# Layer 0 of a two-layer convolution and recurrence kernel: the MLP of a tile moved to other places of the loop, its residual from VectorE to ScalarE and GpSimd

## The chip, the cores and the metric

The kernel runs on one core of a Trainium2 chip. The metric is the device time of one execution in microseconds (us), and lower is better. The engines are PE (TensorE, the matrix engine), DVE (VectorE), ACT (ScalarE), POOL (GpSimd) and SP, which starts the loads and stores. Each has a queue of its own, which it works off in order; engines wait for one another by semaphores.

## What is computed

The input is x with 16 images of 16 x 16 tokens and 96 channels. Two layers follow one another. Layer 0, cut to what matters:

```python
h = layernorm(x, n1_g, n1_b)
p = h @ w_in + b_in                              # 96 -> 192 channels
local = depthwise_conv_3x3(p, k_conv)
lr, rl = ema(local, axis=2), ema(local, axis=2, reverse=True)
tb, bt = ema(local, axis=1), ema(local, axis=1, reverse=True)
mixed = layernorm(0.25 * (lr + rl + tb + bt) + local, on_g, on_b)
x = x + (mixed @ w_out + b_out)                  # 192 -> 96
h2 = layernorm(x, n2_g, n2_b)
x = x + gelu(h2 @ w1 + b1) @ w2 + b2             # 96 -> 384 -> 96
```

Layer 1 is a layer norm, two products (u and a gate g), eight steps of h = g * (h @ A) + (1 - g) * u, a residual, and a second MLP of the same size. The change doesn't touch its code, apart from waits at its start.

## The kernel before

**Tiles.** x is held in SBUF as 8 tiles of two images, 512 tokens each, in four chunks of 128 tokens. Layer 0 is a loop over passes i = -2 to 8 (`body0(i)`, written once for each engine, the first and last passes unrolled). A pass works on several tiles at once, and the names are the same on all engines: n = i + 2 (statistics of the first layer norm, LN1, and its scaling into `xn1`), f = i + 1 (transposes of `xn1` into bank 0, the split of it into a high and a low part `xh1`, `xl1`, and the product with w_in into `pA` or `pM` and bank 1), c = i (the nine taps of the convolution, accumulated in `cA` and `cB`), m = i - 1 (`cA`, `cB` transposed, copied to `local`, the mix of all four scans as a product with the matrix `mix`, its copy `mixed`, six transposes of it, `mcA` and `mcB`, W_out, the residual `x2`, and LN2 into `xn2`), g = i - 2 (transposes of `xn2`, split `xh2`, `xl2`, first MLP product with w1, gelu into `hid`) and e = i - 3 (second MLP product with w2 into bank 7, residual into `x_all`). After pass 8 comes a turn (`turn`), in which the recurrence of tile 0 starts while the last MLPs of layer 0 are finished, and then layer 1's loop.

**PE** (L1310 to L1440 of `body0`) works in each pass through: transposes of `cA`, `cB` (L1333), LN1's transposes (`ln1_transposes`), two thirds of the second MLP product (`mlp2`, L1215), LN2's transposes (`ln2_transposes`), the mix (L1379), the first third of the first MLP product (`mlp1`, L1197 to L1199, three products each: high by high, low by high, high by low), the transposes of `mixed` (L1396, L1398), the second third, W_out (L1414, L1419), the last third, w_in (L1298, L1310), and the first third of `mlp2` of the next tile. In passes 2 and 8 (`mix_first`) LN2's transposes stand behind the mix and the whole of `mlp1` behind W_out.

**ACT** copies from PSUM (`local` L660, `mixed` L698, `mcA` and `mcB` L707 and L708, the splits L536 and L537), scales LN1's output (`normalize1`, L629), applies the first tap (`first_taps`, L650) and the gelus (`gelu0`, L611). One-time work stands between: `setup1` and `setup_m1` in pass 2 (L582 to L595) and `setup2` in pass 3 (L601 to L604).

**DVE** has the statistics (L828, L832, L974, L984), taps 1 to 8 (L933), `x2` (L1002) and the MLP's residual (`residual3`, L874).

**POOL** has the power -0.5 of the variances (`inverse_std`, L367: `rs1`, `rsm`, `rs2`), the low parts of the splits (L364), `xn2` (L374), the additions of a row (`add_row`, L378: `xb` is x plus a bias, used by `x2`; `x_all<-x2,rows` adds the MLP's bias b2), and one-time work (`setup_w1_low` L407, `setup2` L427).

## Time and profile before

| | us |
|---|---|
| Median of 3 runs | 236.05 (235.89 to 236.66) |
| The profiled execution's own time | 236.0 |
| Its span | 234.2 |
| PE busy | 227.3 (97%) |
| DVE busy | 187.3 (80%) |
| ACT busy | 133.5 (57%) |
| POOL busy | 127.7 (55%) |

The profile is of one execution. Its span runs from the first to the last instruction, and 1.8 us of the execution's own time lie around it. Matmuls are pipelined: the profile's duration of one is longer than the distance to the next, so a PE that is busy all the time in the table can still have gaps of some tenths of a us. Where such gaps matter, starts are compared with starts.

The page shows 26% of the chain of work that ended last as "issue", nearly all of it in layer 1, and PE with 43% as the largest engine in it. A line or a time below always belongs to the kernel before, unless it is said otherwise.

### The profile page before, as it was taken

To read this page: it belongs to the slowest core of one execution; us is meant where nothing else is said; L and a number is where in the kernel's file an instruction comes from. 1 tells how busy PE (TensorE), PEld (TensorE's weight loads), DVE (VectorE), ACT (ScalarE), POOL (GpSimd) and SP (SyncE) were. 2 spreads that over 40 slices of the span, in tenths; PEclk is the share of its full clock that TensorE was granted. 3 is DMA by queue.
4 is the path that set the end of the run, shared out by engine and by line. 5 is a ranking of instruction groups with operands and counts; after the bars stand their busy time and mean duration, and the time that the engine had idled before them with its cause. 6 is when DMAs were issued, how large, how long until landed. Compare 5 with 4: busy or idle time off the path is not lost.

```text
span 234.2 us, 4144 instructions
## 1 busy us (share of the span) xinstructions
PE 227.3 (97%) x1376; PEld 184.9 (79%) x1376; DVE 187.3 (80%) x470; ACT 133.5 (57%) x301; POOL 127.7 (55%) x161
## 2 busy tenths in 40 slices
PE   8999899999999999999999999999999999999995
PEld 5796867969697978887787887878788887978685
DVE  7799998999999999995458688696968778686741
ACT  5667886767675866455923937264372727353252
POOL 6564777887859392938677351526335351516130
PEclk9999999999999999999999999999999999999999
DMA  3951000000000000000000000010101001010102
GB/s 107 231 168 36 1 0 0 4 0 0 3 1 0 3 1 0 3 0 0 0 3 1 0 3 0 0 35 4 34 1 34 3 0 34 3 34 0 35 3 67
DMA packets 5637, 4.99 MB, mean 21 GB/s; under 512 B 528, under 2 KB 5360, under 8 KB 5616
## 3 DMA queue, kind: packets, MB, share of 16 engines
q1 hardware_dynamic: 5328, 4.64, 6.9%
q8 instruction: 11, 0.18, 0.3%
q10 hardware_dynamic: 288, 0.09, 0.2%
q14 instruction: 10, 0.08, 0.1%
HBM read 3.15 MB, written 1.57 MB: 20 GB/s over the span
## 4 chain that ended last, share of the span: by engine, by line
PE 43%; issue 26%; POOL 17%; DMA 5%; DVE 5%; ACT 2%; SPq 1%; POOLq 0%; DVEq 0%; ACTq 0%
PE pM L1215 8%; PE bank L1379 8%; POOL hs L493 8%; POOL rs L367 6%; DMA x_all<-in_x 5%; PE bank L1414 3%; POOL x4b L378 3%; PE pM L1197 3%; PE bank L1184 3%; PE bank L1419 2%; PE bank L1333 2%; PE bank L1310 2%; PE pM L1199 2%; PE pM L1198 2%; DVE cA L933 2%
## 5 line engine op out<-in xcount | busy, mean ns | idle before, releaser
L367 POOL TENSOR_TENSOR rs<-var,power 128x4 f32<-128x4 f32 x32 | 32.5, 1016 | 47.4 <-DVE var L832 43.9
L933 DVE SCALAR_TENSOR_TENSOR cA<-pA,cols,cA 128x528 f32<-128x528 f32 x54 | 40.8, 756 | 0.4
L1514 PEld LDWEIGHTS pM<-w,hid 128*128 128x128 f32 x168 | 27.3, 191 | 3.5
L1260 PE MATMUL pA<-q,a_half 96*96 96x256 f32 x96 | 27.1, 381 | 0.3 <-DVE q L1015 0.3
L1514 PE MATMUL pM<-w,hid 128*128 128x96 f32 x168 | 26.9, 263 | 0.0
L933 DVE SCALAR_TENSOR_TENSOR cB<-bank,cols,cB 128x256 f32<-128x256 f32 x56 | 26.5, 473 | 0.0
L1015 DVE SCALAR_TENSOR_TENSOR q<-th,bank 96x256 f32<-96x256 f32 x48 | 19.8, 416 | 7.6 <-PE bank L1260 7.3
L1215 PEld LDWEIGHTS pM<-w,hid 128*128 128x128 f32 x192 | 24.4, 192 | 0.9
L1215 PE MATMUL pM<-w,hid 128*128 128x96 f32 x192 | 24.8, 271 | 0.0
L1184 PE MATMUL bank<-ident,xn 128*96 128x128 f32 x120 | 23.3, 273 | 0.0
L364 POOL TENSOR_TENSOR xl<-xc,xh 96x512 fp32r<-96x512 f32 x15 | 19.1, 1275 | 5.7 <-ACT xh L537 4.8
L1379 PE MATMUL bank<-local,mix 128*128 128x384 f32 x64 | 22.1, 488 | 0.0
L809 ACT ACTIVATE xh<-bank 96x512 fp32r<-96x512 f32 x7 | 4.2, 593 | 26.6 <-PE bank L1184 26.6
L611 ACT ACTIVATE hid<-pM,bias 128x512 f32<-128x512 f32 x23 | 15.2, 688 | 5.9 <-PE pM L1199 5.6
L1379 PEld LDWEIGHTS bank<-local,mix 128*128 128x128 f32 x64 | 11.6, 190 | 6.7 <-issue 0.2
L1184 PEld LDWEIGHTS bank<-ident,xn 128*96 128x96 f32 x120 | 14.9, 136 | 1.9 <-issue 0.6
L1260 PEld LDWEIGHTS pA<-q,a_half 96*96 96x96 f32 x96 | 13.2, 163 | 3.1 <-DVE q L1015 1.1
L1015 DVE SCALAR_TENSOR_TENSOR q_three<-th,pA 96x256 f32<-96x256 f32 x16 | 6.7, 417 | 10.7 <-PE pA L1260 9.7
L493 POOL TENSOR_TENSOR hs<-hs,q_three 96x512 f32<-96x512 f32 x8 | 10.2, 1270 | 9.0 <-DVE q_three L1015 9.0
L374 POOL TENSOR_SCALAR xn<-x,ng,rs 128x96 f32<-128x96 f32 x32 | 13.1, 424 | 1.7 <-POOL rs L367 1.6
L1015 DVE SCALAR_TENSOR_TENSOR q<-th,pA 96x256 f32<-96x256 f32 x32 | 12.6, 413 | 1.5 <-PE pA L1260 0.8
L698 ACT ACTIVATE mixed<-bank 128x384 f32<-128x384 f32 x16 | 7.9, 491 | 9.1 <-PE bank L1379 9.1
(245 smaller groups left out, 579.7 us busy)
## 6 DMA issues: line engine op xcount, KB each, us to landing
x_all<-in_x SPq DMA_DIRECT2D x8, 192.0 KB, 2.9
out<-y SPq DMA_DIRECT2D x7, 192.0 KB, 2.0
w<-in_w SPq DMA_DIRECT2D x1, 480.0 KB, 6.0
w<-in_w SPq DMA_DIRECT2D x1, 336.0 KB, 3.3
mix<-in_mix SPq DMA_DIRECT2D x1, 256.0 KB, 3.5
out<-y SPq DMA_DIRECT2D x2, 96.0 KB, 1.7
...
```

Source lines behind the costliest of these rows:

```text
L364: return pool.tensor_tensor(lo[0:D, :], v[0:D, :], hi[0:D, :].bitcast(F32), ALU.subtract)
L367: pool.tensor_tensor(rs[:, :], var[:, :], power[:, :], ALU.pow).then_inc(step, 1)
L374: pool.tensor_scalar(xn[:, k * D:(k + 1) * D], v[:, k * D:(k + 1) * D], ng[:, k:k + 1], rs[:, k:k + 1], ALU.add, ALU.mult).then_inc(ready, 1)
L493: pool.tensor_tensor(hs[c % 2][0:D, :], hs[c % 2][0:D, :], moved(c, k)[0:D, :], ALU.add)\
L611: act.activation(hid[:, j * TILE:(j + 1) * TILE], bank[banks[j]][:, :], ACT.Gelu, bias=B[f"b1_{j}"]).then_inc(s["gelu_done"], 1)
L933: dve.scalar_tensor_tensor(out=acc, in0=src, scalar=col(f"k{'AB'[grp]}{k}"), in1=acc, op0=ALU.mult, op1=ALU.add).then_inc(s["conv_step"], 1)
L1015: dve.scalar_tensor_tensor(out=moved(c, k + 1)[0:D, half(h)], in0=th[c % 2][0:D, half(h)], scalar=1.0, in1=step_bank(k, h), op0=ALU.add, o ...
L1184: last = pe.transpose(dst[0:D, k * P:(k + 1) * P], src[:, k * D:(k + 1) * D], ident[:, :])
L1215: last = pe.matmul(psum[:, k * D:(k + 1) * D], hid[:, j * TILE + k * P:j * TILE + (k + 1) * P], wc0("w2", j * D, (j + 1) * D), start=(j == ...
L1260: pe.matmul(step_bank(k, h), a_half[0:D, :], moved(c, k)[0:D, half(h)], start=k not in (1, 3), stop=True, skip_group_check=True)\
L1379: last = pe.matmul(bank[4 + a][:, 0:384], mix[:, k * TOKENS + a * P:k * TOKENS + (a + 1) * P], local[:, k * 384:(k + 1) * 384], start=(k = ...
L1514: last = pe.matmul(bank[V_BANK][:, k * D:(k + 1) * D], hid1[:, j * TILE + k * P:j * TILE + (k + 1) * P], wc1("m2", j * D, (j + 1) * D), st ...
```

## The change

**What it does.** In layer 0's loop:

- PE: LN2's transposes move behind the mix in all passes. `mlp1` moves to the end of the pass, behind W_out and w_in, and its third part goes to bank 0 instead of bank 6. Inside `mlp1` the product with `xl2` comes third instead of second, with the wait for `xl2` in front of it. `mlp2` is no longer begun in the pass before: its 12 chunk products (24 matmul instructions in the trace) are put between the LN1 transposes, the halves of the mix, the LN2 transposes, and four of them behind the transposes of `mixed`. `ln2_bank` is bank 6 instead of bank 0.
- Since the third part of `mlp1` is in bank 0, LN1's transposes (bank 0 too) wait for the third gelu of the tile (`gelu_done`), and so do layer 1's first transposes in pass 8 (`ln3_transposes(0)`).
- ACT: `normalize1` moves forward, behind the split of the tile f and, in pass 2, ahead of `setup1`. The split of `xn2` moves behind `mcB`, and the three gelus to the end of the pass, behind `first_taps`. `mcA` waits for the first four transposes of `mixed` only. A new copy of bank 7 to `xr` follows `mcB`.
- POOL: `rs1` moves to the start of the pass, `xb` is made in the pass that uses it, `xl2` moves behind `rsm` (and, in pass 3, behind `setup2`), and a new addition `x_all<-xr,x_all` follows.
- DVE: the residual L874 leaves layer 0's loop (it stays for the last two tiles, which are finished in the turn and behind it).

The core of the diff:

```diff
         def ln2_bank(t):
-            return bank[1 if t >= TILES - 2 else 0]
+            return bank[1 if is_last(t) else 6]
...
@@ POOL, body0 @@
-                if peeled(i, 1):
+                if tile_known(n) and not peeled(i, 0):
                     ln1_std()
...
-                if tile_known(g):
-                    pool.wait_ge(s["x2_split"], 2 * g + 2)
-                    wait(pool, s["hid_psum"], 3 * g)
-                    split_low(xl2, xc2, xh2).then_inc(s["x2_lo"], 1)
+                if tile_known(m):
+
+                    pool.wait_ge(*x_landed(m))
...
+                    wait(pool, s["x2_ready"], 4 * m)
+                    add_row(xb[:, :], x_tile(m), brow[:, :], s["xb_ready"])
...
                     if peeled(i, 3):
                         setup2()
+                    if tile_known(g):
+                        ln2_low()
+                    if tile_known(e):
+                        pool.wait_ge(s["xr_ready"], e + 1)
+                        pool.wait_ge(s["x2b_ready"], e + 1)
+                        pool.tensor_tensor(x_tile(e), xr[:, :], x_tile(e), ALU.add).then_inc(s["x3_ready"], 1)
...
@@ ACT, body0 @@
+                if i >= 2:
+                    normalize1(n)
                 if peeled(i, 2):
                     setup1()
                     setup_m1()
...
+                if tile_known(e) and i <= TILES:
+                    act.wait_ge(s["w2_done"], e + 1)
+                    wait(act, s["x3_ready"], e)
+                    act.activation(xr[:, :], bank[7][:, 0:384], ACT.Copy).then_inc(s["xr_ready"], 1)
+                if tile_known(g) and not is_last(g):
+                    split2()
...
@@ DVE, body0 @@
-                if tile_known(e):
-                    residual3(e, bank[7])
...
@@ PE, body0 @@
+                    if f >= 4:
+                        pe.wait_ge(s["gelu_done"], 3 * (f - 3))
...
+                if tile_known(g) and not is_last(g):
+                    if peeled(g, 0):
+                        pe.wait_ge(s["w1_high"], 2)
+                        pe.wait_ge(s["w1_low"], 1)
+                    mlp1(g, 0, bank[6])
+                    wait(pe, s["xr_ready"], g)
+                    mlp1(g, 1, bank[7])
+                    if peeled(i, TILES):
+                        pe.wait_ge(s["x3_lo"], 1)
+                    else:
+                        pe.wait_ge(s["x2_ready"], 4 * m + 4)
+                    mlp1(g, 2, bank[0])
```

**Where the order moves.** On POOL, from the end of pass 1 to the middle of pass 2, this stands before (`xn2` here is tile 0's, the last `rs1` tile 4's):

```order
L378 TENSOR_TENSOR xb<-x_all,brow 128x384 [waits brow_ready,wo_ready]
L367 TENSOR_TENSOR rs1<-var1,power 128x4 [waits xn1_ready,var1_ready]
L364 TENSOR_TENSOR xl1<-xc1,xh1 96x512 [waits p_psum,x1_split]
L367 TENSOR_TENSOR rsm<-varm,power 128x4 [waits varm_ready]
L407 TENSOR_TENSOR w1_l<-w1_f,w1_h 96x384 [waits w1_high]
L370 TENSOR_TENSOR ng2<-st2,minus 128x4 [waits var2_ready]
L367 TENSOR_TENSOR rs2<-var2,power 128x4
L374 TENSOR_SCALAR xn2<-x2,ng2,rs2 128x96 [waits ln2_step]
L374 TENSOR_SCALAR xn2<-x2,ng2,rs2 128x96 x3
L378 TENSOR_TENSOR xb<-x_all,brow 128x384 [waits x2_ready,x_odd_loaded]
L364 TENSOR_TENSOR xl1<-xc1,xh1 96x512 [waits p_psum,x1_split]
```

And in the changed kernel:

```order
L364 TENSOR_TENSOR rs1<-var1,power 128x4 [waits xn1_ready,var1_ready,wo_ready]
L361 TENSOR_TENSOR xl1<-xc1,xh1 96x512 [waits p_psum,x1_split]
L375 TENSOR_TENSOR xb<-x_all,brow 128x384 [waits brow_ready,x_even_loaded]
L364 TENSOR_TENSOR rsm<-varm,power 128x4 [waits varm_ready]
L404 TENSOR_TENSOR w1_l<-w1_f,w1_h 96x384 [waits w1_high]
L367 TENSOR_TENSOR ng2<-st2,minus 128x4 [waits var2_ready]
L364 TENSOR_TENSOR rs2<-var2,power 128x4
L371 TENSOR_SCALAR xn2<-x2,ng2,rs2 128x96 [waits ln2_step]
L371 TENSOR_SCALAR xn2<-x2,ng2,rs2 128x96 x3
L364 TENSOR_TENSOR rs1<-var1,power 128x4 [waits xn1_ready,var1_ready]
L361 TENSOR_TENSOR xl1<-xc1,xh1 96x512 [waits p_psum,x1_split]
```

`xb` of tile 0 now stands between `xl1` and `rsm`, and tile 4's `rs1` right behind tile 0's `xn2`.

On ACT, pass 2, from the split of tile 3 to the copy of the mix, the changed kernel has this. Before, the two rows of `xn1` stood behind the first two gelus, and the others were in this order:

```order
L544 ACTIVATE xh1<-bank0 96x2x2x128
L636 ACTIVATE xn1<-x_all,rs1 128x96 [waits trx_done,x_even_loaded,ln1_step]
L636 ACTIVATE xn1<-x_all,rs1 128x96 x3
L589 ACTIVATE a_half<-w1 96x96 [waits w1_loaded]
L593 ACTIVATE bias<-pM,cols 96x1 [waits l1_psum]
L593 ACTIVATE bias<-pM,cols 96x1
L596 ACTIVATE bias<-pM,cols 128x1 x3
L598 ACTIVATE ug_f<-pM 96x192
L602 ACTIVATE m1_f<-pM 96x384 [waits l1_psum]
L707 ACTIVATE mixed<-bank4 128x384 [waits mix_done,varm_ready,mtr_done]
L707 ACTIVATE mixed<-bank5 128x384 [waits mix_done]
```

`ln1_step` is what `rs1` on POOL signals, so the six one-time copies and both `mixed` now stand behind a wait for POOL.

On PE, pass 7, the changed kernel has this at the end, from the last W_out product to the transposes of pass 8; before, two of the three MLP parts stood ahead of W_out and the third right behind it:

```order
L1442 MATMUL bank0<-woBB,mcB 128x2x96
L1217 MATMUL pM<-xh2,w1_h 128x512 [waits gelu_done,x2_split]
L1218 MATMUL pM<-xh2,w1_l 128x512
L1221 MATMUL pM<-xl2,w1_h 128x512 [waits x2_lo]
L1217 MATMUL pM<-xh2,w1_h 128x512 [waits xr_ready]
L1218 MATMUL pM<-xh2,w1_l 128x512
L1221 MATMUL pM<-xl2,w1_h 128x512
L1217 MATMUL bank0<-xh2,w1_h 128x512 [waits x2_ready]
L1218 MATMUL bank0<-xh2,w1_l 128x512
L1221 MATMUL bank0<-xl2,w1_h 128x512
```

In passes 2 to 6 the twelve products of w_in (L1315, L1327 there) stand between W_out and these rows; in pass 7 there are none, since no tile is left for w_in.

## Rows read from the trace of the kernel before

**Rows 1.** Busy time by window, one a pass: length, then each engine's, then granted clock.

```profile
27.63:41.99 14.36, 13.45 (x86) 10.79 (x84) 13.59 (x36) 10.52 (x28) 9.82 (x14) 1.00 0.00 1
41.99:55.22 13.23, 13.21 (x88) 10.81 (x86) 12.66 (x31) 9.53 (x24) 10.88 (x15) 1.00 0.00 1
...
68.21:81.23 13.02, 13.02 (x87) 10.84 (x86) 12.38 (x29) 8.94 (x19) 9.21 (x13) 1.00 0.01 2
...
94.23:105.30 11.07, 11.07 (x72) 8.93 (x70) 10.97 (x25) 5.63 (x12) 7.29 (x10) 1.00 0.01 1
105.30:117.64 12.34, 12.06 (x74) 9.50 (x73) 6.03 (x17) 8.86 (x22) 8.40 (x11) 1.00 0.00 0
```

**Rows 2.** PE's timeline in pass 5: start us, us, operation.

```profile
68.21 0.60 PE L1333 MATMUL bank<-ident,cA 128*128 128x128 f32 x4
...
68.86 0.60 PE L1184 MATMUL bank<-ident,xn 128*96 128x128 f32 x4
...
74.27 0.51 PE L1197 MATMUL pM<-xh,w_h 96*128 96x512 f32 x1
...
76.59 1.13 PE L1414 MATMUL bank<-woA,mcA 128*128 128x96 f32 x8
...
78.93 0.41 PE L1298 MATMUL pA<-xh,wi_h 97*128 97x256 f32 x2
...
80.37 1.03 PE L1215 MATMUL pM<-w,hid 128*128 128x96 f32 x8
81.23 0.49 PE L1333 MATMUL bank<-ident,cA 128*128 128x128 f32 x3
```

**Rows 3.** ACT's timeline in pass 5.

```profile
79.13 0.69 ACT L611 ACTIVATE hid<-pM,bias 128x512 f32<-128x512 f32 x1
```

**Rows 4.** DVE's timeline in pass 5.

```profile
71.33 0.56 DVE L874 TENSOR_TENSOR x_all<-pM,x_all 128x384 f32<-128x384 f32 x1
...
78.53 0.99 DVE L1002 SCALAR_TENSOR_TENSOR x<-bank,rsm,xb 128x96 f32<-128x96 f32 x4 [0.31 <-PE bank L1419]
```

**Rows 5.** POOL's timeline in passes 1 and 2.

```profile
25.38 1.01 POOL L367 TENSOR_TENSOR rsm<-varm,power 128x4 f32<-128x4 f32 x1
...
29.88 1.66 POOL L374 TENSOR_SCALAR xn<-x,ng,rs 128x96 f32<-128x96 f32 x4
31.51 1.00 POOL L378 TENSOR_TENSOR xb<-x_all,brow 128x384 f32<-128x384 f32 x1
```

**Rows 6.** ACT's timeline in pass 2.

```profile
30.25 0.29 ACT L582 ACTIVATE a_half<-w 96x96 f32<-96x96 f32 x1
...
31.34 0.53 ACT L595 ACTIVATE m_f<-pM 96x384 f32<-96x384 f32 x1
...
33.49 0.49 ACT L698 ACTIVATE mixed<-bank 128x384 f32<-128x384 f32 x1 [0.72 <-PE bank L1379]
```

**Rows 7.** DVE's timeline in pass 2.

```profile
34.38 0.55 DVE L974 BATCH_NORM_STATS2 stm<-mixed 128x6 f32<-128x384 f32 x1
...
37.64 0.75 DVE L933 SCALAR_TENSOR_TENSOR cA<-pA,cols,cA 128x528 f32<-128x528 f32 x1
```

**Rows 8.** The one-time work of pass 3 on ACT.

```profile
50.55 0.29 ACT L601 ACTIVATE bias<-bias 96x1 f32<-96x1 f32 x2
...
50.99 0.51 ACT L604 ACTIVATE m_h<-m_f 96x384 fp32r<-96x384 f32 x1
```

**Rows 9.** The same on POOL, and a low part of the split.

```profile
52.16 1.01 POOL L427 TENSOR_TENSOR m_l<-m_f,m_h 96x384 fp32r<-96x384 f32 x1
...
72.94 1.27 POOL L364 TENSOR_TENSOR xl<-xc,xh 96x512 fp32r<-96x512 f32 x1 [0.24 <-ACT xh L537]
```

**Rows 10.** ACT's timeline at the change from pass 7 to pass 8.

```profile
105.22 1.16 ACT L753 ACTIVATE xn<-x_all,rs 128x96 f32<-128x96 f32 x4
```

**Rows 11.** PE's timeline in layer 1, where transposes and pairs of products alternate.

```profile
133.00 0.27 PE L1184 MATMUL bank<-ident,xn 128*96 128x128 f32 x1
...
133.31 0.27 PE L1184 MATMUL bank<-ident,xn 128*96 128x128 f32 x1
```

More of the change, by code:

```diff
@@ L177, in build @@
         xb, x2 = sb("xb", CHUNKS * D), sb("x2", CHUNKS * D)
+        xr = sb("xr", CHUNKS * D)
         hid = sb("hid", HJ * TILE)
@@ L436, in ln1_std, with ln2_low @@
                     inverse_std(rs1, var1, s["ln1_step"])
-                if peeled(i, 1):
+                def ln2_low():
+                    pool.wait_ge(s["x2_split"], 2 * g + 2)
+                    wait(pool, s["hid_psum"], 3 * g)
+                    split_low(xl2, xc2, xh2).then_inc(s["x2_lo"], 1)
+                if tile_known(n) and not peeled(i, 0):
                     ln1_std()
@@ L1206, in mlp1 @@
                 w = slice(P * j, P * (j + 1))
-                three_passes(psum[:, :], w1_h[0:D, w], w1_l[0:D, w], xh2[0:D, :], xl2[0:D, :])\
-                    .then_inc(s["hid_psum"], 1)
+                pe.matmul(psum[:, :], w1_h[0:D, w], xh2[0:D, :], start=True, stop=False)
+                pe.matmul(psum[:, :], w1_l[0:D, w], xh2[0:D, :], start=False, stop=False)
+                if j == 0:
+                    pe.wait_ge(s["x2_lo"], g + 1)
+                pe.matmul(psum[:, :], w1_h[0:D, w], xl2[0:D, :], start=False, stop=True)\
+                  .then_inc(s["hid_psum"], 1)
             def mlp2(e, j, psum, parts=range(CHUNKS)):
@@ L1316, in body0, with last_mlp @@
                 f, m, g, e = i + 1, i - 1, i - 2, i - 3
+                def last_mlp(*places):
+                    for at in places:
+                        if tile_known(e):
+                            mlp2(e, at // CHUNKS, bank[7], [at % CHUNKS])
                 if peeled(i, -2):
                     keep_warm(WARM_UP)
-                if tile_known(e):
-                    mlp2(e, 0, bank[7])
                 if tile_known(m):
@@ L1352, in ln1_transposes @@
                     else:
-                        transposes(bank[0], xn1, s["trx_done"])
+                        for k in range(CHUNKS):
+                            transposes(bank[0], xn1, s["trx_done"], [k])
+                            between(k)
                 if peeled(i, 0):
@@ L1361, in body0 @@
                 elif tile_known(f):
-                    ln1_transposes()
+                    ln1_transposes(last_mlp)
+                else:
+                    for k in range(CHUNKS):
+                        if peeled(i, TILES):
+                            ln3_transposes(0, [k])
+                        last_mlp(k)
                 if peeled(i, 2):
@@ L1365, in body0 @@
                     setup2()
-                if tile_known(e):
-                    mlp2(e, 1, bank[7])
-                    mlp2(e, 2, bank[7])
-                if peeled(i, TILES):
-                    ln3_transposes(0)
-                if tile_known(g) and not mix_first(g):
-                    ln2_transposes(g)
                 if tile_known(m):
@@ L1384, in body0 @@
                     ln1_transposes()
-                if mix_first(g):
-                    ln2_transposes(g)
-                mlp1_now = tile_known(g) and not is_last(g)
-                if mlp1_now and not mix_first(g):
-                    mlp1(g, 0, bank[6])
+                for k in range(CHUNKS):
+                    if tile_known(g):
+                        ln2_transposes(g, [k])
+                    if k < 2:
+                        last_mlp(6 + k)
                 if tile_known(m):
@@ L1395, in body0 @@
                             k = 2 * im + a
-                            pe.transpose(bank[4][:, k * P:(k + 1) * P], src, ident[:, :])
+                            last = pe.transpose(bank[4][:, k * P:(k + 1) * P], src, ident[:, :])
+                    last.then_inc(s["mtr_done"], 1)
                     for a in range(2):
@@ L1403, in body0 @@
                     gu(0, 1)
-                if mlp1_now and not mix_first(g):
-                    wait(pe, s["x3_ready"], g)
-                    mlp1(g, 1, bank[7])
                 if tile_known(m):
```

82 lines of the change are left out of this document (36 added, 46 removed).

## The prediction, made before the changed kernel was run

> **What bounds the kernel now.** I read the windows first, pass by pass, then PE's timeline inside one pass, then the rows of the other engines at the places where PE waits. A full pass of layer 0 takes 13.02 us and PE is busy in all of it, the clock granted in full; DVE has 12.38 us of it [rows 1]. So layer 0 is PE's. Comparing starts shows what little is left: in pass 5 PE waits about 0.08 us for LN2's transposes, 0.21 us before the first MLP part at 74.27 and 0.25 us before W_out at 76.59 [rows 2]. That is 0.54 us, so PE's own work in a full pass is 12.48 us. DVE is close behind but does wait for PE: 0.31 us before `x2` [rows 4]. By the same comparison of starts PE's gaps in passes 2 to 8 are 1.65, 0.75, 0.51, 0.54, 0.52, 0.47 and 0.75 us, together 5.2 of the 90.0 us from the first to the last of these windows. Layer 1 follows at its own pace, and its recurrence starts as soon as PE has worked off pass 8. What passes 2 to 8 gain or lose is therefore gained or lost in the end.
>
> **The removed and added work.** No matmul is added or taken away. DVE loses one residual a tile for six tiles, 0.56 us each [rows 4], which counts nothing while DVE waits for PE. ACT gets a copy of 128x384 from PSUM, 0.49 us like that of the mix [rows 6], and POOL an addition of 128x384, between 1.00 (one operand a repeated row, [rows 5]) and 1.27 us (two full operands of 96x512, [rows 9]); I take 1.0. In a middle pass both have room for it. Twelve chunk products now alternate with transposes and mix halves. The nearest rows are layer 1's, a transpose and two trace instructions of a product in 133.31 - 133.00 = 0.31 us [rows 11], against 0.11 + 2 x 0.11 = 0.33 from groups of one kind (0.60 us of transposes take 0.44 by starts; eight instructions 81.23 - 80.37 = 0.86 [rows 2]). So alternating costs nothing; between -0.02 and +0.02 us each it is 0.2 us a pass at most either way.
>
> The Trainium skill (SBUF — State Buffer, on the two separate sides) says that a GpSimd instruction and a VectorE instruction with two SBUF inputs hold one port pair in turn and block each other. By that rule an addition of two SBUF tiles on POOL might hold DVE up by up to its 1.0 us. In layer 0 DVE's taps and `x2` read one operand from PSUM, so the rule asks nothing here, and by it the sum is the same.
>
> **Where the waits go, pass by pass.** I use four latencies, as starts show them: PE's end to ACT's start 0.20 us (the MLP part ends where the next product starts, 78.93, and the gelu starts at 79.13 [rows 2, 3]), ACT's end to PE about 0.1, POOL to ACT or PE 0.05 to 0.1, PE to DVE 0.3.
>
> *Middle passes (4, 5, 6; the same wait also in 3 and 8).* `mlp1` is now last in the pass, and its third part is in bank 0, which LN1's transposes of the next pass need. Between them PE has only the transposes of `cA` and `cB`, 68.86 - 68.21 = 0.65 us. The third gelu starts 0.20 us after the third part, lasts 0.69 [rows 3], and PE goes on about 0.09 later: 0.98 us after the end of `mlp1`, a wait of 0.33. ACT is free for the gelus, since the taps' copies end 0.2 us earlier. The other waits are covered. The low part of the split is asked for 3.4 us after `mlp2`'s end, and xr 0.2 + 0.49, split 1.1, `xl2` 1.27 make 3.1; the copy `mixed` (0.2 + 0.49 after the mix) is under 0.88 us of LN2 transposes and products; `mcA` is under the last four products. DVE's tap 8 ends about 0.9 us before w_in asks. So 12.48 + 0.33 = 12.81 us a pass, and three passes gain 0.2 each: **-0.6**.
>
> *Pass 2.* This is the largest term. `xn1` of tile 4 now stands on ACT ahead of `setup1` and of `mixed`, and waits for `rs1`, which stands on POOL behind tile 0's `xn2`. `xn2` needs `x2`, `x2` needs `rsm`, and `xb` (1.0 us, about 0.6 of it new delay) is put ahead of `rsm`: it started at 25.38 [rows 5] and now at 26.0, so `x2` and all after it come 0.4 later. `xn2` ended at 31.5 and now at 32.0; `rs1` takes 1.0: 33.0. Then ACT: `xn1` 1.1 (34.1), the six one-time copies from 30.25 to 31.34 + 0.53, so 1.6 (35.7), two `mixed` 0.9 (36.6). The second `mixed` ended at 33.98 [rows 6]: 2.6 later. PE, done with the mix at 33.3, stands until 35.8 for LN2's transposes (bank 6 must have been read by `setup1`), then takes the transposes of `mixed` at 36.65 and W_out at 38.0, done at 39.6. DVE waits for `mixed` too: its statistics start at 36.2, and tap 8 on `cA` ends 37.64 + 0.75 - 34.38 = 4.0 later [rows 7], at 40.2. w_in starts at 40.3 instead of right behind W_out. With 1.42 of w_in and 2.1 of `mlp1` the pass ends at 43.84. Before, it ended at 41.99 with 0.87 of `mlp2` in it that is now in pass 3; that compares 43.84 with 41.12: **+2.7**.
>
> *Pass 3.* `setup2` stands on ACT behind the copy to `xr` and the split, and on POOL ahead of `xl2`. From 43.84 on: `mlp2` ends at 51.56 (with the gelu's wait of 0.33), `xr` 51.76 to 52.25, the split to 53.2, on ACT `setup2` (50.99 + 0.51 - 50.55 = 0.95 [rows 8]) to 54.1, on POOL `ug_l` and `m1_l` (1.0 [rows 9], from 54.3) to 55.3 and `xl2` to 56.6. PE comes to the first product with `xl2` at 55.0 and gets it at 56.7: 1.7 of wait. With 0.33 that is 2.05 against 0.75 before: **+1.3**.
>
> *Pass 7.* There is no w_in any more, so `mlp1` comes right behind W_out while its split has only just begun: `mlp2` ends at 7.3 us of the pass, W_out at 8.85, the split at 9.05 (`xr` is ahead of it), `xl2` at 10.4. PE waits 0.35 for the split and 0.9 for the low part. The late gelu also delays `local` and with it the mix by 0.35. Together 1.6 against 0.47: **+1.1**.
>
> *Pass 8.* Layer 1's first transposes wait for their `xn3`, which ACT makes behind the three gelus. The gelus are now last in pass 7: 0.20 + 0.69 after the pass ends, then 1.16 for the four scalings [rows 10] less the 0.1 by which neighbours overlap, so PE goes on 2.04 us into the pass, where it would have been there at 0.65. All of `mlp2` stands behind these transposes. 1.4 against 0.75 before, since the old gap at the MLP goes: **+0.6**.
>
> **The sum** is -0.6 + 2.7 + 1.3 + 1.1 + 0.6 = +5.1, unrounded +5.2. The recurrence starts at about 122.8 instead of 117.64 [rows 1]. Against the profiled execution's own 236.0 us that is 241.2; the median 236.05 is the same within its spread.
>
> **Rivals.** (1) *DVE was the real pace.* If the 0.56 us residual counts in full, passes 3 to 6 fall by 0.54 each (PE's own work is the floor) and the added waits are passed under other work: 236.0 - 2.2 = 233.8, faster. For it speaks that DVE has 12.38 of 13.02 us; against it the 0.31 us that DVE waits for PE, and that the waits in passes 2, 3, 7 and 8 follow from the queues' order. It decides if `rs1` of tile 4 is there when ACT has done the split in pass 2 (30.4); my chain has it at 33.0, so 2.6 us would have to be wrong. (2) *The waits at the end don't bind:* the copy to `xr`, split and low part in pass 7 are ready sooner, or what pass 8 loses is given back in the turn, where PE, DVE and POOL alternate: without the 1.7 us of passes 7 and 8, and with a middle pass of 12.6, 239.0. (3) *The clock falls.* PE stands 2.5 us in pass 2, where before no gap in a pass was above 0.7, and the granted clock was 1.00 in every window [rows 1]. At half the clock the 7 us of PE work that follow cost up to 3.5 more: 244; a middle value is 243.5. The Trainium skill (TensorE: Matmul & The Clock Gate, part 1) has it that the throttled rate is the default and that activity releases it; no run here shows it yet, and by that page a long enough stand in pass 2 would give just this. (4) *Nothing measurable:* pass 2's and 3's waits are half hidden and the middle passes gain more: about 236, which has no mechanism of its own in the rows.
>
> **Chances.** The forecast (239.8 to 242.8) 0.74, rival 2 (238 to 239.8) 0.10, the clock 0.08, rival 1 0.05, rival 4 0.03. The range reaches from 239.2 to 243.0: at its low end most of the waits of pass 7 or 8 are gone, at the high end alternating costs 0.2 a pass and the addition on POOL 1.27. A measurement of this kernel can tell 0.3% (0.7 us) from no change. Faster by more 0.05, within it 0.03, slower 0.92.
>
> **What the changed profile would show.** Passes 4 to 6 at 12.8 us each, with PE's wait for the gelu in front of LN1's transposes; 12.5 would say that the bank's wait is covered, 13.0 that something else came. In pass 2 `rs1` at about 32 on POOL, ACT idle from 30.4 to 33, `mixed` at 35.7 and PE idle from 33.3 to 35.8. In pass 3 a wait of PE for POOL's `xl2` of 1.7 us, in pass 7 one of 0.9, in pass 8 one of 1.4 for ACT's `xn3`. Layer 1's tiles keep their distance. The prediction is wrong if the start of the recurrence moves by less than 3 us, or if layer 1 gets shorter.

## The result, and the profile after

Before: 236.73 us, median of 6 executions (235.89 to 237.09). After: 242.95 us, median of 6 (241.07 to 243.6). The changed kernel takes 1.025 times as long, 95% interval 1.021 to 1.029. The profiled execution of after took 241.07 us, 5.1 more than the one of before; its span is 239.3 us and its granted clock 1.00. In the other executions the clock is lower in most, which is a cost of its own (below).

The windows, one a pass, as in [rows 1] (length, then busy time of PE, its weight loads, DVE, ACT and POOL, then the granted clock). The rows are passes 2, 3, 4, 7 and 8 (5 and 6 are as long as 4):

```profile
28.41:44.02 15.61, 12.77 (x78) 9.85 (x77) 14.23 (x37) 10.00 (x27) 10.39 (x14) 1.00 0.00 0
44.02:58.46 14.44, 12.82 (x87) 10.69 (x86) 13.53 (x33) 10.26 (x25) 11.41 (x15) 1.00 0.01 2
58.46:71.22 12.76, 12.55 (x86) 10.77 (x85) 10.83 (x26) 9.40 (x21) 10.35 (x14) 1.00 0.00 1
...
96.74:108.81 12.07, 11.36 (x71) 8.99 (x69) 11.83 (x29) 6.17 (x13) 8.72 (x13) 1.00 0.01 1
108.81:122.53 13.72, 12.54 (x81) 10.35 (x79) 4.11 (x11) 9.94 (x24) 8.68 (x11) 1.00 0.01 1
```

In a middle pass PE is busy for 12.55 us where it was 13.02, and the pass is 0.26 shorter: the change does there what it is made for. Passes 2, 3, 7 and 8 lose more than that. Where, the list of PE's waits from pass 1 to the end of pass 8 shows (us in total, times, longest):

```profile
PE pM L1221 <- POOL xl L361: 2.0, 2, 1.4
PE pM L1195 <- ACT m_f L602: 1.9, 1, 1.9
PE bank L1195 <- ACT xn L765: 1.2, 1, 1.2
...
PE bank L1195 <- ACT hid L618: 0.9, 4, 0.2
PE bank L1327 <- DVE cB L946: 0.8, 1, 0.8
PE pA L1315 <- DVE cA L946: 0.4, 1, 0.4
```

None of these is in before, but for the waits for `mcA` that are left out here. L1221 is the product with `xl2` in passes 3 and 7, L1195 the transposes: of LN2 in pass 2, of layer 1 in pass 8, of LN1 in passes 3 to 6 (0.2 us by the list, 0.37 by starts).

Pass 2, the largest. POOL's and ACT's timelines in after, then PE's:

```profile
25.06 1.01 POOL L375 TENSOR_TENSOR xb<-x_all,brow 128x384 f32<-128x384 f32 x1
26.17 1.02 POOL L364 TENSOR_TENSOR rsm<-varm,power 128x4 f32<-128x4 f32 x1
...
30.67 1.67 POOL L371 TENSOR_SCALAR xn<-x,ng,rs 128x96 f32<-128x96 f32 x4
32.31 1.00 POOL L364 TENSOR_TENSOR rs<-var,power 128x4 f32<-128x4 f32 x1
```

```profile
33.35 1.17 ACT L636 ACTIVATE xn<-x_all,rs 128x96 f32<-128x96 f32 x4 [2.18 <-POOL rs L364]
...
35.52 0.49 ACT L602 ACTIVATE m_f<-pM 96x384 f32<-96x384 f32 x1
35.90 0.87 ACT L707 ACTIVATE mixed<-bank 128x384 f32<-128x384 f32 x2
```

```profile
36.16 0.62 PE L1195 MATMUL pM<-ident,xn 128*96 128x128 f32 x4 [1.93 <-ACT m_f L602]
...
38.16 1.13 PE L1437 MATMUL bank<-woA,mcA 128*128 128x96 f32 x8 [0.47 <-ACT mcA L714]
...
40.38 0.51 PE L1315 MATMUL pA<-xh,wi_h 97*128 97x256 f32 x2 [0.41 <-DVE cA L946]
```

`xb` now starts where `rsm` started [rows 5], and everything down the chain is later: ACT stands 2.18 us for `rs1` of tile 4, the second `mixed` ends at 36.77 instead of 33.98 [rows 6], and PE, which could go on at 34.2, goes on at 36.16.

Pass 3. `setup2` on POOL (L424) stands ahead of the low part, and PE waits:

```profile
53.86 0.60 POOL L424 TENSOR_TENSOR ug_l<-ug_f,ug_h 96x192 fp32r<-96x192 f32 x1 [1.03 <-ACT ug_h L610]
54.42 1.01 POOL L424 TENSOR_TENSOR m_l<-m_f,m_h 96x384 fp32r<-96x384 f32 x1
55.40 1.26 POOL L361 TENSOR_TENSOR xl<-xc,xh 96x512 fp32r<-96x512 f32 x1
```

```profile
56.71 0.50 PE L1221 MATMUL pM<-xl,w_h 96*128 96x512 f32 x1 [1.40 <-POOL xl L361]
```

And PE in passes 7 and 8:

```profile
107.06 0.51 PE L1221 MATMUL pM<-xl,w_h 96*128 96x512 f32 x1 [0.62 <-POOL xl L361]
...
110.81 0.32 PE L1195 MATMUL bank<-ident,xn 128*96 128x128 f32 x1 [1.18 <-ACT xn L765]
```

The recurrence starts at 122.53 instead of 117.64, +4.89. From there to the end of the span it was 116.56 us and is 116.77, so layer 1 is as it was.

### The profile page after: what moved, and what is told of

Read it like the earlier page. It is cut to its first block, busy times and chain, and to the rows that moved or that the text cites. A ratio compares the mean times of both kernels' runs of the same rounds, so it can differ in the third digit from the quotient of the medians.

```text
span 239.3 us, 4158 instructions
## 1 busy us (share of the span) xinstructions
PE 225.9 (94%) x1376; PEld 184.7 (77%) x1376; DVE 186.1 (78%) x464; ACT 137.0 (57%) x307; POOL 134.0 (56%) x167
## 4 chain that ended last, share of the span: by engine, by line
PE 32%; issue 29%; POOL 23%; DVE 8%; ACT 7%; POOLq 0%; DVEq 0%; ACTq 0%
POOL rs L364 8%; POOL hs L500 7%; PE pM L1229 6%; PE bank L1402 6%; ACT hid L618 4%; POOL x4b L375 3%; DVE cA L946 3%; PE bank L1143 2%; PE bank L1195 2%; PE bank L1437 1%; DVE cB L946 1%; PE bank L1442 1%; POOL xn L371 1%; POOL xl L361 1%; PE bank L1277 1%
## 5 line engine op out<-in xcount | busy, mean ns | idle before, releaser
L1229 PEld LDWEIGHTS pM<-w,hid 128*128 128x128 f32 x192 | 28.4, 192 | 5.2 <-issue 1.2
L1538 PEld LDWEIGHTS pM<-w,hid 128*128 128x128 f32 x168 | 27.3, 191 | 3.5
L1229 PE MATMUL pM<-w,hid 128*128 128x96 f32 x192 | 29.0, 265 | 0.0
L1538 PE MATMUL pM<-w,hid 128*128 128x96 f32 x168 | 26.9, 263 | 0.0
L1402 PE MATMUL bank<-local,mix 128*128 128x384 f32 x64 | 24.6, 497 | 0.1
L1195 PE MATMUL bank<-ident,xn 128*96 128x128 f32 x92 | 21.6, 274 | 2.0 <-ACT xn L765 1.2
L1195 PEld LDWEIGHTS bank<-ident,xn 128*96 128x96 f32 x92 | 12.7, 143 | 4.2 <-issue 1.9
L364 POOL TENSOR_TENSOR rsm<-varm,power 128x4 f32<-128x4 f32 x8 | 8.2, 1019 | 12.8 <-DVE varm L995 12.7
L618 ACT ACTIVATE hid<-pM,bias 128x512 f32<-128x512 f32 x16 | 10.7, 687 | 5.2 <-PE pM L1221 5.0
L1402 PEld LDWEIGHTS bank<-local,mix 128*128 128x128 f32 x64 | 10.7, 191 | 3.8 <-ACT local L667 0.3
```

Source lines behind the costliest of these rows:

```text
L364: pool.tensor_tensor(rs[:, :], var[:, :], power[:, :], ALU.pow).then_inc(step, 1)
L618: act.activation(hid[:, j * TILE:(j + 1) * TILE], bank[banks[j]][:, :], ACT.Gelu, bias=B[f"b1_{j}"]).then_inc(s["gelu_done"], 1)
L1195: last = pe.transpose(dst[0:D, k * P:(k + 1) * P], src[:, k * D:(k + 1) * D], ident[:, :])
L1229: last = pe.matmul(psum[:, k * D:(k + 1) * D], hid[:, j * TILE + k * P:j * TILE + (k + 1) * P], wc0("w2", j * D, (j + 1) * D), start=(j == ...
L1402: last = pe.matmul(bank[4 + a][:, 0:384], mix[:, k * TOKENS + a * P:k * TOKENS + (a + 1) * P], local[:, k * 384:(k + 1) * 384], start=(k = ...
L1538: last = pe.matmul(bank[V_BANK][:, k * D:(k + 1) * D], hid1[:, j * TILE + k * P:j * TILE + (k + 1) * P], wc1("m2", j * D, (j + 1) * D), st ...
```

## The experiments

All runs of a group share their runs of before. Its medians were 236.39 (first group, with `again`, `warm`, `ln1_late`, `xb_back`), 236.15 (second, with `setup2_p4`, `two_ahead`, `tail8`, `tail7`) and 236.66 us (third). Since the granted clock differs from one execution to the next, I give the time at each clock.

**The changed kernel again.**

> The changed kernel itself, to see its spread. Its runs so far fall into two groups, 241.1 to 241.4 us with a mean granted clock of 1.00 and 243.0 to 243.6 us with 0.986 to 0.993. Theory (clock): PE stands about 2.1 us in pass 2, and in some executions the clock then falls for some us; so again two groups, 241.2 and 243.1, and the kernel before shows 1.00 in all its runs. If a profile shows the lower clock, PEclk drops in a stretch that begins near pass 2 (34 to 36 us). Rival (place by chance): the lower clock shows in runs of the kernel before as well, and its place has nothing to do with the stand in pass 2.

Measured: 242.92 us, ratio 1.027 (1.022 to 1.031). One by one: 240.82 at clock 1.00; 242.83, 242.92 and 242.93 at 0.993; 244.24 at 0.984; 245.4 at 0.977. With the first six there are three executions at 1.00 (240.82 to 241.35), four at 0.993 (242.83 to 242.95), four at 0.984 to 0.986 (242.96 to 244.24) and one at 0.977. The profiled one here was at 0.993. In its windows of 1 us (columns as above) the clock is at half, 1.2 GHz, from about 57.4 to 60.8:

```profile
56.00:57.00 1.00, 0.00 (x0) 0.00 (x0) 1.00 (x3) 0.00 (x0) 1.00 (x1) 1.00 0.00 0
57.00:58.00 1.00, 0.82 (x2) 0.70 (x3) 1.00 (x3) 0.06 (x1) 1.00 (x2) 0.68 0.00 0
58.00:59.00 1.00, 1.00 (x4) 0.73 (x3) 1.00 (x3) 0.63 (x1) 1.00 (x3) 0.50 0.00 0
...
60.00:61.00 1.00, 1.00 (x6) 0.80 (x6) 1.00 (x3) 0.56 (x1) 1.00 (x4) 0.62 0.00 0
61.00:62.00 1.00, 1.00 (x10) 0.81 (x9) 1.00 (x3) 0.80 (x3) 0.97 (x2) 1.00 0.00 0
```

Ahead of it stands PE's wait for `xl2` in pass 3, 1.42 us in this trace (56 to 57 holds no matmul at all). So the fall has a place, and I had not named it: my clock rival spoke of pass 2 alone. By the Trainium skill (TensorE: Matmul & The Clock Gate, part 1) the throttled rate is the default and activity releases it. These rows agree: half the clock behind a stand, the full one again with PE busy.

**Pass 2's stand filled with matmuls of no use.**

```
+if peeled(i, 2):
+    pe.wait_ge(s["x1_split"], 8)
+    keep_warm(4, bank[0])
 for k in range(CHUNKS):
     if tile_known(g):
         ln2_transposes(g, [k])
```

> The changed kernel with four matmuls of ones into bank 0 put into PE's stand in pass 2, ahead of LN2's transposes; 4 x 0.43 = 1.7 us of work into 2.1 us of idle time, nothing waits for them. Theory (clock): the granted clock is 1.00 in all runs and the median is that of the fast group, 241.1 us (LN2's transposes start at 36.16 as they do now). Rival: the two groups stay, since the fall comes from something else, and the median stays near 243.

Measured: 241.18 us, ratio 1.022 (1.019 to 1.026). Four executions at 1.00 (240.85 to 241.23) and two at 0.993 (242.85, 242.95); none at 0.986 or below. The stand in front of LN2's transposes is 0.64 us instead of 1.93, PE's times are otherwise the same. The time is the expected one, the full clock in all executions is not there. Six executions alone don't settle which fall belongs to which stand; the profiles of the runs below do: those at 0.993 have one fall behind pass 3's stand, the one at 0.986 one behind pass 2's, those at 0.978 and 0.979 both.

**LN1 of tile 4 in its old place, behind `mixed`.**

```
 act, ahead of the setup:             act, at the end of the pass:
-if i >= 2: normalize1(n)            -if i < 2 and ...: normalize1(n)
+if i >= 3: normalize1(n)            +if i < 3 and ...: normalize1(n)
```

> The changed kernel with one move undone: in pass 2 ACT scales tile 4's LN1 behind the gelu inputs again (ahead of the first taps), not ahead of the one-time copies. My account of pass 2: ACT no longer waits for POOL's rs1 at 30.5 to 33.3, LN2's transposes start at 34.1 instead of 36.2, and then DVE sets the pace: its statistics of the mix start at 35.2 instead of 36.4, w_in at 39.2 instead of 40.4. So 1.2 us less, not 2.1: 239.9 at full clock. PE's longest stand in pass 2 is then below 1 us, so by the clock theory all runs have a clock of 1.00. Rival (the wait doesn't matter, PE's other waits take its place): 241.1.

Measured: 241.11 us, ratio 1.020 (1.018 to 1.022); all four executions at 0.993, with the low clock behind pass 3's stand again (0.74 in 57 to 58, 0.50 in 58 to 59). LN2's transposes start at 34.63 with no wait, and W_out at 36.72. Then one wait has become another:

```profile
36.72 1.13 PE L1437 MATMUL bank<-woA,mcA 128*128 128x96 f32 x8 [0.47 <-ACT mcA L714]
...
39.69 0.50 PE L1315 MATMUL pA<-xh,wi_h 97*128 97x256 f32 x2 [1.16 <-DVE cA L946]
```

Pass 2 takes 43.29 - 28.98 = 14.31 us instead of 15.61, 1.3 less where 1.2 was expected. The median is 1.8 us below `again`'s executions at the same clock; no row here places the 0.5 between the two. The expected gain is there, the expected full clock is not, and DVE's tap leaves a stand of 1.16 us where none above 1 was expected.

**`xb` of tile 0 in its old place, at the end of POOL's pass 0 and ahead of `rsm`.**

```
 pool, ahead of rsm:                  pool, behind setup_w_out() of pass 0:
-if tile_known(m):                        +pool.wait_ge(s["brow_ready"], 1)
+if tile_known(m) and not peeled(m, 0):   +add_row(xb, x_tile(0), brow, s["xb_ready"])
     add_row(xb, x_tile(m), brow, s["xb_ready"])
```

> The changed kernel with tile 0's row addition xb where it was, ahead of rs1 of tile 3 at the end of POOL's pass 0. Theory (port): in the changed kernel DVE's varm of pass 1 lasts 0.90 instead of 0.26 us and ends 0.02 us after POOL's xb (25.06 to 26.07); it is held until that ends. With xb gone from there varm lasts about 0.3 and ends with xl1 on POOL, w_in's second half starts 0.8 us earlier (26.8), x2 of tile 0 starts at 26.7 instead of 27.5, and the whole chain of pass 2 (rs1, LN1's scaling, the mix) comes 0.8 earlier: 240.3 at full clock. Rival (queue only, what I had predicted): rsm alone was late, x2 comes 0.4 earlier, 240.7, and varm keeps its 0.9.

Measured: 240.17, 240.24 and 240.32 us at 1.00, 243.37 and 243.47 at 0.986, 243.82 at 0.977; median 241.85, ratio 1.022 (1.017 to 1.027). At the full clock this is 0.6 to 0.8 us below the changed kernel, and nearer to the 240.3 of the port theory than to its rival's 240.7. `varm` took 0.15 us, which decides between them. `xb` starts at 22.11 (22.05 in the kernel before), `x2` at 26.80 instead of 27.47, and pass 3 at 43.30 instead of 44.02. Three executions of six still fall, as both stands are still there (1.89 and 1.40 us).

**`setup2` on POOL one pass later.**

```
 pool:
+if peeled(i, 4):
+    setup2()
 pool.wait_ge(s["varm_ready"], m + 1)
...
-if peeled(i, 3):
-    setup2()
 ln2_low()
```

> The changed kernel with one thing moved: POOL's setup2 (ug_l and m_l of layer 1) goes from pass 3, ahead of the low part of LN2, to the start of pass 4, ahead of rsm. Theory: in pass 3 the first MLP products wait 1.4 us for POOL's low part, because setup2's two operations stand ahead of it (0.60 and 1.01 us long). Without them that wait is gone, the pass is about 12.9 instead of 14.4 us, and the whole is 1.6 us shorter: 239.4 us at the clock of 1.00 (the changed kernel at that clock: 240.8 to 241.4). Pass 4 gets nothing, because POOL waits for varm there. The same stand of PE in pass 3 is what the clock falls behind in the executions at 0.993, so fewer of them should fall than of the changed kernel: most at 1.00, the rest with one fall and 241.3. Rival: POOL is then late for rsm of pass 4 by 1.6 us, x2 and with it the product W_out come later, and the time only moves from pass 3 to pass 4: 241.0 us.

Measured: 239.58 us, ratio 1.017 (1.012 to 1.021); five executions at 0.998 to 1.00 (239.23 to 240.26) and one of 242.78 at 0.986. PE goes through the products with `xl2` of pass 3 without a wait, the pass takes 57.44 - 44.69 = 12.75 us instead of 14.44, and pass 4 12.98, 0.2 longer: 1.5 us less in the trace. Against their own runs of before the executions at the full clock are 3.3 us above (239.42 - 236.15), `again`'s was 4.4: 1.2 less. Of the rival's return in pass 4 only 0.2 us came. No execution shows 0.993 any more. My price for the one that fell, 241.3, was too low: at 0.986, the mark of a fall behind pass 2's stand, it costs 3.3.

**Two products of the second MLP ahead of LN1's transposes.**

```
-ln1_transposes(last_mlp)
+last_mlp(0, 1)
+ln1_transposes(lambda k: last_mlp(k) if k > 1 else None)
```

> The changed kernel with PE's order of the second MLP product changed: in passes 2 to 7 two of its products stand ahead of LN1's transposes and the rest among them, where all stood among the transposes. Theory: in each middle pass PE waits 0.33 us for the third gelu or for the bank it frees, and two products more ahead of that point hide it: 0.3 us in each of four passes, 1.3 us in all, 239.8 us at a clock of 1.00. Rival: the wait isn't at that place or LN1's transposes now come too late for DVE's copy cA and for the projection behind it: a wait of 0.2 to 0.5 us moves there, 241.0 to 242 us.

Measured: 239.46 us at 0.998; 241.84 at 0.993, 242.89 at 0.986, 243.08 at 0.978; median 242.36, ratio 1.022 (1.016 to 1.027). At the full clock this is 3.3 us above its runs of before, 1.1 less than `again`'s 4.4, where 1.3 was expected. Passes 5 and 6 of its trace:

```profile
73.95:86.35 12.40, 12.40 (x87) 10.81 (x86) 12.15 (x30) 9.54 (x21) 10.30 (x14) 1.00 0.01 3
86.35:98.74 12.39, 12.39 (x87) 10.81 (x85) 11.59 (x29) 8.49 (x17) 9.28 (x13) 1.00 0.00 0
```

A middle pass is 0.37 shorter than after's 12.76, and PE is busy in all of it: the wait for the gelu in bank 0 was real, 0.37 us a pass, and could be covered. In this profile, at 0.978, the clock was at half from 36.0 to 42.9 and again from 59.9 to 63.3, behind both stands. And pass 2's stand is longer than in `after`:

```profile
36.10 1.06 PE L1195 MATMUL pM<-ident,xn 128*96 128x128 f32 x4 [2.38 <-ACT m_f L602]
```

**Six products ahead of layer 1's first transposes in pass 8.**

```
+elif peeled(i, TILES):
+    last_mlp(0, 1, 2, 3, 4, 5)
+    ln3_transposes(0)
```

> The changed kernel with PE's order in pass 8 changed: six of the second MLP products stand ahead of layer 1's first transposes. Theory: PE waits there 1.18 us for ACT's xn of layer 1, and products that don't need it can fill that time: the recurrence starts 1.2 us earlier, 239.8 us at a clock of 1.00. Rival: the products wait for gelu themselves (0.69 us each on ACT, which is behind xn), so that what is gained at the transposes is lost at the products: 241 us.

Measured: 240.2 us at 1.00, 242.0 and 242.07 at 0.993, 244.07 at 0.986; median 242.04, ratio 1.022 (1.018 to 1.026). PE has no wait at these transposes any more, and pass 8 takes 125.51 - 112.69 = 12.82 us instead of 13.72. That is 0.9 of the 1.2 expected. The rest has become the next wait: by starts, PE now stands 0.27 us before the mix, which starts at 115.44, for ACT's `local`, which ends at 115.39. Its profile shows the clock at 0.50 from 39.5 to 46.3, 1.8 us behind pass 2's stand (2.38 us here too), and 1.00 behind pass 3's, which is there too (1.40 us).

**Split and low part first in pass 7.**

```
 act:  +if peeled(i, TILES - 1): split2()     # ahead of the copy to xr
 pool: +if peeled(i, TILES - 1): ln2_low()    # ahead of rsm
```

> The changed kernel with two operations moved in pass 7: on ACT LN2's split stands ahead of the residual's copy, on POOL LN2's low part ahead of rsm. Theory: PE waits 0.62 us for POOL's low part, and more for the split behind the mix, since both stand behind other work; with both moved up these waits go, 0.6 to 1.1 us, 240.0 us at a clock of 1.00. Rival: rsm, now later by 1.27 us, holds the values of tile 7's x2, and with them its mix and layer 1's beginning: 241 to 242 us.

Measured: 241.41 us at 1.00, three of 243.19 to 243.31 at 0.992 to 0.993; median 243.24, ratio 1.027 (1.023 to 1.031). No gain, and pass 7 takes 111.05 - 98.57 = 12.48 us instead of 12.07. The rival held:

```profile
106.86 1.28 POOL L361 TENSOR_TENSOR xl<-xc,xh 96x512 fp32r<-96x512 f32 x1 [3.40 <-ACT xh L546]
108.10 1.01 POOL L364 TENSOR_TENSOR rsm<-varm,power 128x4 f32<-128x4 f32 x1
109.20 0.99 DVE L1017 SCALAR_TENSOR_TENSOR x<-bank,rsm,xb 128x96 f32<-128x96 f32 x4 [1.42 <-POOL rsm L364]
110.25 0.50 PE L1221 MATMUL bank<-xh,w_h 96*128 96x512 f32 x1 [0.86 <-DVE x L1017]
```

`rsm` comes later, `x2` with it, and the third part of `mlp1` waits for `x2`. Whichever of the two POOL does first, PE waits for the other.

**The residual alone, in the kernel before.**

```
 dve:  -residual3(e, bank[7])
 act:  +act.activation(xr, bank[7][:, 0:384], ACT.Copy)
 pool: +pool.tensor_tensor(x_tile(e), xr, x_tile(e), ALU.add)
 pe:   wait(pe, s["x3_ready"], g)  ->  wait(pe, s["xr_ready"], g)
```

> The kernel before with the third part of the change alone: the residual's sum leaves DVE, ACT copies bank 7 to SBUF and POOL adds x. PE's order and everything else as before. Theory: in a middle pass DVE waits for PE (0.31 us ahead of x2) and PE never waits for DVE, so 0.56 us less on DVE brings nothing, and the two operations put on ACT and POOL cost nothing either, as both have idle time: 236.2 us, within 0.5. Rival: DVE is what a pass waits for, 0.56 us in each of four passes: 234.0 us. Second rival: POOL's 1.0 us in front of LN2's step makes PE wait for xn, a few tenths a pass: 237 to 238 us.

Measured: 236.87 us, ratio 1.0024 (0.9998 to 1.0050). A middle pass is as it was in [rows 1], with DVE 0.43 us less busy:

```profile
69.11:82.10 12.99, 12.99 (x87) 10.84 (x87) 11.95 (x28) 9.41 (x20) 10.21 (x14) 1.00 0.01 3
```

DVE is not what layer 0 waits for, and this third of the change gains nothing.

**Pass 2's stand filled and `setup2` moved.**

> The changed kernel with setup2 in pass 4 and the four matmuls without use in pass 2's stand. Theory: the clock falls behind the stands of PE in pass 2 and pass 3 and nowhere else; with both filled or gone all six executions show 1.00, and the time is that of setup2_p4 at that clock, 239.3 to 239.7 us. Rival: falls have another cause (the chip, the moment), then one or two of the six show 0.993 or 0.986 here too, at 1.9 us each.

The edits are those of `warm` and of `setup2_p4`. Measured: 240.11 us, ratio 1.015 (1.012 to 1.018), all five executions at 1.00 (239.27 to 240.24). With the 0.5 us by which before was slower here than beside `setup2_p4` taken off this is 239.6, within the expected 239.3 to 239.7. With the stands filled or gone, no execution of this kernel falls, nor one of `five_moves` below. They are not the only cause there is: before itself showed 0.979 and 0.978 in two of its 45 executions of the three groups (241.96 and 242.09 us), and the residual alone 0.993 in one of twelve.

**POOL's addition with one SBUF input.**

```
-pool.tensor_tensor(x_tile(e), xr, x_tile(e), ALU.add)
+pool.tensor_scalar(x_tile(e), xr, 1.0, None, ALU.mult)
```

> The changed kernel with POOL's sum of the residual turned into an operation with one SBUF input (xr times 1, so the sum with x is left out) in the same place. DVE's var2 runs beside it in passes 3 to 7, and took 0.64, 0.39 and 0.38 us where it takes 0.15 to 0.17 alone, with its end at the end of POOL's operation. Theory: a DVE operation from SBUF to SBUF is held until POOL's running operation ends because that one reads two SBUF inputs; with one input it isn't held, and var2 takes 0.15 to 0.17 us in every pass. Rival: any POOL operation holds it, or it waits for something else: 0.4 to 0.6 us stays. The whole time tells nothing here.

The kernel leaves out x in the sum, so its result is wrong and its time tells nothing (one execution, 244.1 us at 0.979). What it is about: DVE's `varm` and `var`, a tensor_scalar of 128x4 from SBUF to SBUF, take 0.15 to 0.17 us. In after, the one at the end of pass 1 took 0.90, and one in each of passes 3 to 7 took 0.38 to 0.64. DVE's rows of after:

```profile
25.19 0.90 DVE L995 TENSOR_SCALAR varm<-stm 128x4 f32<-128x4 f32 x1
...
95.31 0.39 DVE L844 TENSOR_SCALAR var<-st 128x4 f32<-128x4 f32 x1
```

The first ends at 26.09, POOL's `xb` (in the rows of pass 2 above) at 26.07. The last ends at 95.70, and POOL's addition, in its timeline, at 95.67:

```profile
94.65 1.02 POOL L477 TENSOR_TENSOR x_all<-xr,x_all 128x384 f32<-128x384 f32 x1
```

The kernel before had the hold already, 0.1 us of it, at the end of pass 1, DVE's operation ending 0.04 behind POOL's:

```profile
25.05 0.26 DVE L984 TENSOR_SCALAR varm<-stm 128x4 f32<-128x4 f32 x1
```

```profile
24.00 1.27 POOL L364 TENSOR_TENSOR xl<-xc,xh 96x512 fp32r<-96x512 f32 x1
```

Measured with one input: `var` takes 0.17 us in the middle of POOL's operation in passes 4 to 7. Pass 5, DVE and POOL:

```profile
85.54 0.17 DVE L844 TENSOR_SCALAR var<-st 128x4 f32<-128x4 f32 x1
```

```profile
84.92 1.18 POOL L477 TENSOR_SCALAR x_all<-xr 128x384 f32<-128x384 f32 x1
```

One `var` in the same trace fell beside POOL's `m_l` (56.22 to 57.22) and `xl2`, both with two SBUF inputs:

```profile
57.12 1.35 DVE L844 TENSOR_SCALAR var<-st 128x4 f32<-128x4 f32 x1
```

```profile
57.19 1.26 POOL L361 TENSOR_TENSOR xl<-xc,xh 96x512 fp32r<-96x512 f32 x1
```

It ends at 58.47, POOL's at 58.45. So it is held until a POOL addition or subtraction of two full tiles from SBUF ends, and not by one with a single input. The number of inputs alone doesn't decide, though. After has a `var` inside POOL's power of 128x4, which has two SBUF inputs and lasts 1.02 us, and it isn't held:

```profile
96.26 0.17 DVE L844 TENSOR_SCALAR var<-st 128x4 f32<-128x4 f32 x1
```

```profile
95.92 1.02 POOL L364 TENSOR_TENSOR rs<-var,power 128x4 f32<-128x4 f32 x1
```

Whether the small size or the operation makes that difference, no run separates.

Nor is `varm` held in each execution: it depends on which of the two starts first. In the profiles of `after`, `again`, `ln1_late`, `setup2_p4`, `tail7` and `warm_p4` it starts 0.13 to 0.16 us behind `xb` and takes 0.87 to 0.90 us; in those of `warm`, `tail8` and `one_input` it starts 0.14 to 0.21 ahead of it, in `two_ahead` at the same time within 0.01, and takes 0.15 to 0.29. What the hold costs at the end of pass 1 is little: in `warm` POOL's `xb` started later (25.45), `varm` took 0.28, and from the start of pass 1 to that of pass 3 it is 44.07 - 16.87 = 27.20 us against 44.02 - 16.50 = 27.52 in after. 0.3 us, of the 0.8 by which pass 2 starts late.

**Five moves together.**

> The changed kernel with five moves together, each of them tried alone before: LN1 of pass 2 kept in the old place (ln1_late), the first tile's xb behind rsm (xb_back), setup2 in pass 4 (setup2_p4), two products of the second MLP ahead of LN1's transposes (two_ahead), six ahead of layer 1's first transposes in pass 8 (tail8). Theory: the costs lie in different places and add up. From 241.0 us of the changed kernel at a clock of 1.00: 1.7 less in pass 2, perhaps 0.4 more of xb, 1.5 for setup2, 1.5 for the products, 0.85 in pass 8: 235.1 us, and with no long stand of PE left the clock stays at 1.00 in nearly all executions. Rival: the moves overlap, since a wait that is taken away shows the next one behind it, and half is kept: 238 us.

The edits are those of `ln1_late`, `xb_back` (`xb` at the end of pass 0, so ahead of `rsm` and not behind it), `setup2_p4`, `two_ahead` and `tail8`. Measured: 235.65 us, median of 12 executions (235.13 to 236.33), ratio to before 0.9959 (0.9939 to 0.9978), the clock at 0.998 to 1.00 in all twelve. Passes 2 to 4, 7 and 8:

```profile
28.62:43.04 14.42, 12.54 (x77) 9.89 (x76) 14.21 (x37) 10.08 (x27) 10.36 (x14) 1.00 0.00 0
43.04:55.45 12.41, 12.41 (x87) 10.82 (x85) 11.89 (x29) 10.29 (x25) 10.06 (x13) 1.00 0.01 2
55.45:68.04 12.59, 12.59 (x86) 10.79 (x85) 12.45 (x31) 9.53 (x21) 12.00 (x16) 1.00 0.00 1
...
92.86:104.94 12.08, 11.37 (x71) 8.99 (x70) 11.84 (x29) 6.18 (x13) 8.73 (x13) 1.00 0.01 1
104.94:117.76 12.82, 12.71 (x80) 10.48 (x79) 4.09 (x11) 9.90 (x24) 8.69 (x11) 1.00 0.00 1
```

This is the only kernel here that beats before, by 0.4%, which is little but clear of its interval, and it is some 7 us below the median of the changed one. The costs lay in different places and nearly add up (5.4 us below the changed kernel at the full clock, both against their own runs of before, where 5.95 was expected). Passes 3 to 6 are now 0.4 to 0.8 us shorter than before's, together 2.4. Passes 2 and 8 can't be compared by their windows: before began each tile's second MLP product in the pass ahead (0.87 us), so its pass 2 had that part more than this one's and its pass 8 that part less. With it moved, pass 8 is 12.82 us against 13.21, 0.4 shorter, and pass 2 14.42 against 13.49, 0.9 longer. Pass 7 is 1.0 longer, and so the three give 1.5 of the 2.4 back. Pass 2 is DVE's: it is busy for 14.21 of 14.42 us, and PE waits 1.26 for its tap.

## Why the prediction was right, and where it wasn't

The forecast was 241.2 us in 239.2 to 243.0; the median is 242.95. It is inside by 0.05 us, and that is luck: the high end was explained by 0.2 us a pass for alternating and by an addition of 1.27 us on POOL, and neither came (the middle pass is 12.76, the addition 1.02). The 0.74 was given to 239.8 to 242.8, and the median lies above that, on the way to the clock rival's 243.5. An execution at the full clock takes what was forecast (240.82, 241.07 and 241.35). The rest is the clock, which the forecast itself did not contain. Step by step, at the full clock, with the predicted lengths of passes 3, 7 and 8 worked out from the lengths before and the forecast's terms (pass 8's with the 0.87 us of `mlp2` that is now in it):

| | predicted, us | measured, us |
|---|---|---|
| Start of pass 2 | 27.63 | 28.41 |
| Start of pass 3 (term +2.7) | 43.84 | 44.02 (+2.9) |
| Length of pass 3 (+1.3) | 14.5 | 14.44 (+1.2) |
| Middle pass (-0.6 for three) | 12.81 | 12.76 (-0.7) |
| Length of pass 7 (+1.1) | 12.2 | 12.07 (+1.0) |
| Length of pass 8 (+0.6) | 13.8 | 13.72 (+0.5) |
| Start of the recurrence | 122.8 | 122.53 |
| Layer 1 | as before | +0.2 |

- **Middle passes: right.** PE's own work was taken as 12.48 and the wait for the third gelu as 0.33. `two_ahead` has passes of 12.40 and 12.39 without the wait, and the wait is 0.37.
- **Pass 2: right in mechanism and within 0.2 us, with one thing missed.** The chain was forecast link by link: `rs1` done 33.0 (33.31), `mixed` 35.7 (35.90), PE back at 35.8 (36.16), W_out 38.0 (38.16), w_in 40.3 (40.38). Undoing either link gave its part: `ln1_late` and `xb_back`. One statement in it was wrong: that nothing of the shared port is asked for in layer 0, since taps and `x2` read PSUM. DVE's `varm` and `var` go from SBUF to SBUF, and `xb`, moved beside `varm`, holds it for 0.75 us. I had looked at DVE's long operations and not at its short ones, though before's row of `varm` showed 0.26 us where 0.15 is usual. Where `varm` is held it delays the start of pass 2 by 0.8 us; but POOL's chain of `rsm`, `xn2` and `rs1` sets the end of the pass, and 0.3 of it is left there. So PE's stand is 1.93 us with the hold, and without it 2.38, near the 2.5 of the forecast. In passes 3 to 7 the hold costs nothing that PE sees.
- **Pass 3: right.** The wait was put at 1.7 and is 1.40; moving `setup2` away from it brought 1.5 in the trace.
- **Passes 7 and 8: right** by the term, each 0.1 less than forecast. In pass 7 PE waits, by starts, 0.15 us for the split, 0.78 for the low part and 0.3 before the mix, where 0.35, 0.9 and 0.35 were forecast; in pass 8 1.18 by the list, 1.34 by starts, where 1.4 was. `tail7` shows that pass 7's loss isn't the place of one operation on POOL.
- **The residual: right** that it costs and brings nothing.
- **The clock: wrong in its chance and in its place.** It was given 0.08 and priced at 2.3 to 2.8 us behind pass 2's stand (243.5 to 244; the 3.5 it names would make 244.7). It falls in 9 of 12 executions. Behind pass 3's stand of 1.4 us it costs 1.7 to 2.4 us, behind pass 2's some 2 to 3.9 (after 2 to 3.2, `xb_back` 3.2, `setup2_p4` 3.3, `tail8` 3.9), and no step asked what the 1.7 us of pass 3, which the forecast itself had, would do to it. The step that failed is the rival's argument: a stand of 2.5 us where before had none above 0.7, with nothing in the rows on how the clock takes it, was unknown ground, and such ground is no reason for a small chance. Rival 3 and the forecast should have shared the weight, and the forecast then was about 242 to 243.
- **Rivals 1, 2 and 4** are out: `resid_only` against the first, the waits of 0.62 and 1.18 us in passes 7 and 8 against the second, the interval against the fourth.
